# A gated linear-attention decoder layer in fp32 precision on one core: GpSimd no longer waits for VectorE's split before it prepares the decay exponents

## The chip, the cores and the metric

The kernel runs on one core of a Trainium2 chip. The metric is device time in microseconds (us) of one execution, lower is better. The kernel before took 2335.89 us, the median of three runs (2335.0 to 2343.12).

## The reference, cut to what matters

```python
# x: (4, 512, 512); attention: H = 16 heads, DK = 96, DV = 192
q, k, v = (causal_conv_silu(h @ W) for W in (Wq, Wk, Wv))      # h = layernorm(x)
q, k = l2norm(q) * DK ** -0.5, l2norm(k)
beta = sigmoid(h @ Wb) * 2
g = -exp(A_log) * softplus(h @ Wa + dt_bias)
...
def step(S, inp):                                              # over the 512 tokens
    q_t, k_t, v_t, g_t, b_t = inp
    S = S * exp(g_t)
    delta = (v_t - einsum('bhk,bhkv->bhv', k_t, S)) * b_t
    S = S + einsum('bhk,bhv->bhkv', k_t, delta)
    o = einsum('bhk,bhkv->bhv', q_t, S)
...
x = x + (o * rsqrt(mean(o * o) + eps) * norm_weight * silu(h @ Wg)) @ Wo
x = x + choose_two_sets_and_mix(layernorm(x), ctx_2048, itok)
x = x + bit_linear(silu(bit_linear(y, gate)) * bit_linear(y, val), out)   # y = layernorm(x)
```

The token recurrence is computed in chunks of 128 tokens. Within a chunk the decays between two tokens are exponentials of differences of running sums of g.

## The kernel before, in words

There are three stages. The first normalizes x, the third chooses the sets and does the feed-forward part. The second, `stage_delta_rule`, is the long one: 64 steps numbered n = 0 to 63, one for each of 16 heads and 4 chunks of 128 tokens, each for all four batch rows at once. `c` is the chunk of the step, n modulo 4. In a step the kernel works on four steps' data at once: it projects and convolves q, k, v of step n + 2 (`projection`, `tap0`, `conv`, `tanh`, `silu`), prepares and inverts the triangular matrix of step n + 1, runs the state update of step n, and normalizes, gates and projects the output of step n - 1.

Each engine has its own instruction list, written out by hand, and executes it strictly in order; semaphores (`then_inc`, and `wait_ge` or `past`) order the engines against each other. `past(engine, name, value)` waits until the semaphore has reached the value, and does nothing for a value of zero or less.

These are the pieces around the change:

- GpSimd (`pool`), in a step: `key_decay` makes UB, Em and kinv (L762 to L769); then four products K2 (L823, one of 128x96 for each batch row); then `exponents(n + 2)` (L742), two products of a 128x512 constant with the high and the low half of the f16 pair that holds g, into the one buffer `Gm`; then `values` (L777), two products that make V of the next step from the transposed tokens, after a wait for all four of ScalarE's token copies (`tok_read`); then `epsq` (L832).
- `exponents` itself first waits for `dif_done`, the signal of the two matmuls on TensorE (`exponent_sums`, L884) that read the last `Gm`. They run near the start of a step; the new `Gm` is read near the start of the step after it.
- VectorE: after the state terms `d_V` (L1559) comes `gated`, four products of d_O, the row scale and d_gate into d_on (L1616); `recursion(0)` to `(3)`, four tiny steps on 32 partitions (L1524 to L1534); `silu(0)` (L1473 into d_yv); then `low` (L1624, L1625), which subtracts the f16 high half in d_ohl from d_on and signals `low_ready`; then two taps of the next convolution (L1452), `recursion(4)` (L1536), the third tap, for c other than 2 a small correction (L1458), and `recursion(5)` (the first two L1545).
- In a step with c = 0 VectorE also splits a weight tile (`low_g`, L1441) ahead of `gated`; with c = 2 another (`low_a`, L1436) after `recursion(6)`.
- ScalarE: after the second token copy (L1255) comes `high` (L1350), which waits for d_on and writes the f16 high half; then `tap0(1)` (L1206); then `copy_yj` (L1296), which copies a triangular block that TensorE's `x_join` (L960) waits for; and so on.
- TensorE: ..., `x_join`, `queries` times the state, the fourth token transpose (L875), `turn_output` (L999), which waits for `low_ready` and transposes d_ohl, the rest of the third projection (L859), the output matmuls (L1019), the gates (L974) and the update (L986). The L986 that works on d_V writes a bank that `add_x` (L1630) on VectorE must have read.

The line that the change touches stands in GpSimd's `step`, between K2 and `exponents`:

```python
if st.project:
    past(pool, "low_ready", n)
    exponents(n + 2)
```

Of the kernel before, what the change touches and what calls it, by code (L numbers as in the profile page):

```python
# [79 lines left out]
def over(ap, axis, n):  # L80

    a = ap.unsqueeze(axis)
    shape = list(a.shape)
    shape[axis] = n
    return a.broadcast_to(shape)
# [387 lines left out]
def set_scale(nc, pool, s, c, smv, var, rstd, half):  # L473

    nc.gpsimd.tensor_scalar(var[:, c, :], smv[:, :, :].rearrange("p (b c) m -> p c b m", c=CH)[:, c, :, 1], LN_EPS, None,
                            ALU.add).then_inc(s["var_ready"], 1)
    pool.wait_ge(s["var_ready"], c + 1)
    nc.gpsimd.tensor_tensor(rstd[:, c, :], var[:, c, :], half[:, :], ALU.pow).then_inc(s["rstd_ready"], 1)


def set_weights(nc, pool, s, c, eg, first, second, wt):

    pool.wait_ge(s["eg_ready"], c + 1)
    pool.wait_ge(s["hit_ready"], 2 * c + 2)
    nc.gpsimd.tensor_tensor(second, second, over(eg, 2, NSET), ALU.mult).then_inc(s["wt_ready"], 1)
    pool.wait_ge(s["wt_ready"], 2 * c + 1)
    nc.gpsimd.tensor_tensor(wt[:, c, :, :], first, second, ALU.add).then_inc(s["wt_ready"], 1)
# [39 lines left out]
def stage_delta_rule(nc, io, keep):  # L527
# [6 lines left out]
    with ExitStack() as ctx:  # L534
# [72 lines left out]
        def chosen(c):  # L607
            flat, hits = st[:, c * 320:], y[c][:, :, :].rearrange("p b t -> p (b t)")
            return {"score": flat[:, 0:B * NSET].rearrange("p (b n) -> p b n", b=B),
                    "top": flat[:, 256:288].rearrange("p (b e) -> p b e", b=B),  # L610
                    "topi": st[:, 640 + c * 32:672 + c * 32].bitcast(U32).rearrange("p (b e) -> p b e", b=B),
                    "idx": flat[:, 288:296].rearrange("p (b e) -> p b e", b=B),
                    "gap": flat[:, 296:300], "eg": flat[:, 300:304], "den": flat[:, 304:308],
                    "first": [hits[:, 0:256].rearrange("p (b n) -> p b n", b=B)] * 2,
                    "second": [hits[:, 256:512].rearrange("p (b n) -> p b n", b=B)] * 2}
# [8 lines left out]
        def hold(eng, sem, value):  # L624

            eng.wait_ge(sem, value)
            if not isinstance(value, int):
                eng.sem_inc(held[str(eng.engine)], 1)

        def past(eng, name, value):  # L630

            if not isinstance(value, int):
                if eng.engine == nc.vector.engine:
                    eng.wait_ge(s[name], value)
                else:
                    hold(eng, s[name], value)
            elif value > 0:
                eng.wait_ge(s[name], value)
# [98 lines left out]
        def _(pool):  # L737
            def exponents(n):

                past(pool, "dif_done", n)  # L740
                for w in range(2):
                    nc.gpsimd.tensor_tensor(Gm[:, w, :, :], over(U, 1, B), over(gh[:, w, n, :], 2, P), ALU.mult).then_inc(s["Gm_ready"], 1)  # L742

            def carry(st):

                m = st.n + 2
                past(pool, "tail_done", 3 * m)
                for back in (3, 2, 1):
                    w = over(over(cw[:, st.kp, :, 3 - back], 2, B), 3, back)
                    if back == 3:  # L750
                        nc.gpsimd.tensor_tensor(corr[:, :, :, :], tail[st.pm][:, :, :, :], w, ALU.mult).then_inc(s["corr_ready"], 1)
                        continue
                    past(pool, "corr_ready", 5 * carried(m) + 5 - 2 * back)
                    nc.gpsimd.tensor_tensor(share[:, :, :, 0:back], tail[st.pm][:, :, :, 3 - back:], w, ALU.mult).then_inc(s["corr_ready"], 1)
                    past(pool, "corr_ready", 5 * carried(m) + 6 - 2 * back)
                    nc.gpsimd.tensor_tensor(corr[:, :, :, 0:back], corr[:, :, :, 0:back], share[:, :, :, 0:back], ALU.add).then_inc(s["corr_ready"], 1)

            def key_decay(m, q):

                hold(pool, s["Dn_ready"], 5 * m + 5)  # L760
                past(pool, "Em_ready", m)
                nc.gpsimd.tensor_tensor(UB[:, :, :], over(cst[:, C_NU:C_NU + P], 1, B), over(Dn[:, :], 2, P), ALU.mult).then_inc(s["kappa_done"], 1)  # L762
                nc.gpsimd.tensor_scalar(sse[:, :], nsse[:, :], -1.0, None, ALU.mult).then_inc(s["kappa_done"], 1)
                past(pool, "E_ready", m + 1)
                hold(pool, s["kappa_done"], 4 * m + 2)
                past(pool, "PT_ready", m - 1)
                nc.gpsimd.tensor_tensor(Em[q][:, :, :], E[:, :, :], UB[:, :, :], ALU.mult).then_inc(s["Em_ready"], 1)
                past(pool, "V_ready", m)
                nc.gpsimd.tensor_tensor(kinv[:, :], sse[:, :], phalf[:, :], ALU.pow).then_inc(s["kappa_done"], 1)  # L769
# [18 lines left out]
            def step(st):  # L788
                n, m, c = st.n, st.n + 1, st.c
                if st.output:  # L790

                    past(pool, "ssq_done", B * n)
                    nc.gpsimd.tensor_scalar(ms[:, :], sso[:, :], NORM / DV, None, ALU.mult).then_inc(s["r_ready"], 1)  # L793
                    past(pool, "r_ready", 3 * n - 2)
                    nc.gpsimd.tensor_tensor(ms[:, :], ms[:, :], epsq[st.pm][:, :], ALU.add).then_inc(s["r_ready"], 1)
                    past(pool, "r_ready", 3 * n - 1)
                    past(pool, "on_ready", B * n - B)
                    nc.gpsimd.tensor_tensor(rn[:, :], ms[:, :], mhalf[:, :], ALU.pow).then_inc(s["r_ready"], 1)
                if n >= NS - 1:
                    for at in (0, 1) if n == NS - 1 else (2,):  # L800
                        past(pool, "aggr", B * at + B)
                        set_scale(nc, pool, ss_, at, smv, set_var, set_rstd, mhalf)
                if n == NS:
                    for at in range(2):
                        t = chosen(at)
                        set_weights(nc, pool, ss_, at, t["eg"], t["first"][0], t["second"][0], wt)
                if st.project:
                    if st.cp:
                        carry(st)
                    if not st.recur:  # L810
                        exponents(n + 2)
                    if n == -2:
                        pool.wait_ge(s["set_in"], 96)
                        nc.gpsimd.tensor_copy(bqb[:, :, :], over(bq[:, :], 2, P)).then_inc(s["const_ready"], 1)
                if st.turn:
                    key_decay(m, st.pm)
                if st.recur:

                    past(pool, "su_done", 2 * n)
                    if n == 0:  # L820
                        pool.wait_ge(s["set_done"], 1)
                    for i in range(B):
                        nc.gpsimd.tensor_scalar(K2[:, i, :], tok[st.p][:, i, K_AT:K_AT + DK], Em[st.p][:, i, P - 1:P], None,  # L823
                                                ALU.mult).then_inc(s["K2_ready"], 1)
                    if st.project:
                        past(pool, "low_ready", n)
                        exponents(n + 2)
                if st.turn:

                    values(m, st.pm)  # L830
                    past(pool, "ss_done", B * m + B)
                    nc.gpsimd.tensor_scalar(epsq[st.pm][:, :], ss[:, :], EPS, EPS * DK * NORM, ALU.add, ALU.mult).then_inc(s["kappa_done"], 1)  # L832
                if c == 0 and st.recur:
                    low_o(st.k, st.wk)
                if n == 0:
                    pool.wait_ge(s["set_read"], 3)
                    nc.gpsimd.tensor_scalar(sc[:, NEG, :, :], sc[:, EG, :, :], -1.0, None, ALU.mult).then_inc(s["const_ready"], 1)

            nc.gpsimd.memset(ones[:, :], 1.0).then_inc(s["const_ready"], 1)
            hold(pool, s["const_ready"], 15)  # L840
            all_steps(step)

        @block.tensor
# [1467 lines left out]
```

## Time and profile before

| | before |
|---|---|
| median of 3 runs | 2335.89 us (2335.0 to 2343.12) |
| the profiled execution, its own time | 2335.0 us |
| its span, first to last instruction | 2333.2 us |
| mean granted TensorE clock | 0.984 |
| TensorE matmuls busy | 2250.7 us, 96% |
| VectorE busy | 2074.5 us, 89% |
| ScalarE busy | 1450.8 us, 62% |
| GpSimd busy | 1062.0 us, 46% |

PE is TensorE, PEld its weight loads, DVE VectorE, ACT ScalarE, POOL GpSimd. Times in a timeline are us from the start of the span. A line of it is one instruction or a run of equal ones ("x4"), with the time from the first one's start to the last one's end; in square brackets is how long the engine was idle before it, and who released it.

### The profile page before, as it was taken

The numbers are of one execution on the slowest core, as the hardware profiler recorded it, in microseconds if no ns is written. First come the engines' busy times: TensorE is split into PE (matmuls) and PEld (weight loads), VectorE is DVE, ScalarE is ACT, GpSimd is POOL, SyncE is SP. The second block draws the span as 40 slices with busy tenths as digits, with TensorE's granted clock in tenths as the row PEclk, the third lists the DMA queues.
The fourth block names the chain that finished last, engine by engine and source line by source line (L and its number), as shares of the span: only waits on it lengthen the run. The fifth ranks groups of instructions, "written<-read, shape, count | busy, mean of one in ns | idle before, by whom it ended". The sixth has DMA issues, their size and how long they took to land. (4 is left out here: it accounts for less than half of the span.)

```text
span 2333.2 us, 55508 instructions
## 1 busy us (share of the span) xinstructions
PE 2250.7 (96%) x19873; PEld 1573.5 (67%) x19896; DVE 2074.5 (89%) x4579; ACT 1450.8 (62%) x3955; POOL 1062.0 (46%) x1542
## 2 busy tenths in 40 slices
PE   5899999999999999999999999999999999888998
PEld 3577777777777767777767677777777677763454
DVE  8999999999999999999999998999999989657876
ACT  5566666666666666666666766665656565434665
POOL 3535444444535454535354544445354535214554
PEclk8999999999999999999999999999999999898999
DMA  5211122222212112222221222221111111011000
GB/s 143 62 36 51 50 56 55 57 55 55 51 51 49 53 48 66 63 65 62 56 53 50 65 63 66 64 65 39 34 37 34 22 39 23 17 59 83 24 24 28
DMA packets 289390, 120.76 MB, mean 52 GB/s; under 512 B 211510, under 2 KB 267094, under 8 KB 288604
## 3 DMA queue, kind: packets, MB, share of 16 engines
q1 hardware_dynamic: 289116, 117.21, 19.2%
q8 instruction: 159, 2.61, 0.5%
q14 instruction: 115, 0.94, 0.1%
HBM read 85.42 MB, written 31.74 MB: 50 GB/s over the span
## 5 line engine op out<-in xcount | busy, mean ns | idle before, releaser
L1452 DVE SCALAR_TENSOR_TENSOR d_y<-bank,d_cw,d_y 128x508 f32<-128x508 f32 (+2 forms) x576 | 421.4, 732 | 6.1 <-ACT d_y L1206 1.2
L793 POOL TENSOR_SCALAR d_ms<-d_sso 128x4 f32<-128x4 f32 x64 | 14.5, 226 | 563.8 <-ACT d_junk L1345 563.8
L742 POOL TENSOR_TENSOR d_Gm<-cst,gh 128x512 f16<-128x512 f32 x128 | 131.0, 1044 | 216.5 <-DVE d_ohl L1625 214.5
L1630 DVE SCALAR_TENSOR_TENSOR x<-bank,x 128x512 f32<-128x512 f32 x256 | 172.0, 676 | 43.7 <-PE bank L1019 43.7
L1330 ACT ACTIVATE d_thg<-bank 128x384 f32<-128x384 f32 x128 | 62.2, 486 | 205.1 <-PE bank L974 202.8
L1206 ACT ACTIVATE d_y<-bank,d_cw 128x512 f32<-128x512 f32 x192 | 131.2, 684 | 88.3 <-PE bank L859 86.6
L777 POOL TENSOR_TENSOR d_V<-d_tok,d_kinv 128x640 f32<-128x640 f32 (+1 forms) x128 | 132.0, 1051 | 49.4 <-issue 47.3
L823 POOL TENSOR_SCALAR d_K<-d_tok,d_Em 128x96 f32<-128x96 f32 x256 | 152.1, 609 | 0.1
L1255 ACT ACTIVATE d_tok<-bank 128x384 f32<-128x384 f32 x256 | 125.5, 490 | 36.2 <-PE bank L875 32.3
L1213 ACT ACTIVATE d_th<-d_y 128x512 f32<-128x512 f32 x192 | 122.1, 636 | 39.8 <-DVE d_y L1458 29.8
L1473 DVE SCALAR_TENSOR_TENSOR d_yv<-d_th,d_y 128x512 f32<-128x512 f32 x128 | 89.0, 696 | 52.3 <-ACT d_th L1213 44.5
L1019 PE MATMUL bank<-d_wo1h,d_onT 128*128 128x512 f16 x384 | 131.0, 382 | 3.0 <-ACT d_onT L1357 2.8
L1019 PE MATMUL bank<-d_wo0h,d_onT 128*128 128x512 f16 x384 | 130.1, 380 | 0.2
L1545 DVE TENSOR_TENSOR d_prod<-d_Lb,d_XTb 32x64 f32<-32x64 f32 (+1 forms) x192 | 127.0, 685 | 0.1
L974 PE MATMUL bank<-d_wgh,hhi 128*128 128x192 f16 x1024 | 126.5, 246 | 0.0
L974 PE MATMUL bank<-d_wgl,hhi 128*128 128x192 f16 x1024 | 126.5, 246 | 0.0
L974 PE MATMUL bank<-d_wgh,hlo 128*128 128x192 f16 x1024 | 126.5, 246 | 0.0
L1335 ACT ACTIVATE d_Dl<-bank 128x384 f32<-128x384 f32 x128 | 62.7, 491 | 100.7 <-PE bank L986 100.7
L1345 ACT ACTIVATE d_junk<-d_O 128x192 f32<-128x192 f32 x256 | 89.6, 351 | 53.6 <-DVE d_O L1576 39.5
L986 PE MATMUL bank<-d_V,d_XT 128*128 128x192 f32 x512 | 109.8, 337 | 8.2 <-DVE x L1630 8.2
L832 POOL TENSOR_SCALAR d_epsq<-d_ss 128x4 f32<-128x4 f32 x64 | 25.6, 400 | 199.7 <-ACT d_sq L1308 199.7
L1886 POOL TENSOR_TENSOR f_zv<-f_zv,f_zg 128x512 f32<-128x512 f32 x64 | 83.9, 1312 | 56.3 <-ACT f_zg L2049 34.1
(340 smaller groups left out, 6924.5 us busy)
## 6 DMA issues: line engine op xcount, KB each, us to landing
lt_blocks<-d_LT SPq DMA_DIRECT2D x64, 256.0 KB, 2.5
d_fw<-turned_gate_w SPq DMA_DIRECT2D x32, 256.0 KB, 3.1
d_XT<-x_blocks SPq DMA_DIRECT2D x128, 64.0 KB, 2.3
d_X<-x_blocks SPq DMA_DIRECT2D x128, 64.0 KB, 2.4
d_fw<-turned_val_w SPq DMA_DIRECT2D x32, 256.0 KB, 3.0
d_fw<-turned_out_w SPq DMA_DIRECT2D x32, 256.0 KB, 2.9
d_st<-in_L_attn_Wg_dram SPq DMA_DIRECT2D x16, 384.0 KB, 4.1
ternary<-d_ft SPq DMA_DIRECT2D x48, 128.0 KB, 2.1
```

Source lines behind the costliest of these rows:

```text
L742: nc.gpsimd.tensor_tensor(Gm[:, w, :, :], over(U, 1, B), over(gh[:, w, n, :], 2, P), ALU.mult).then_inc(s["Gm_ready"], 1)
L777: last = nc.gpsimd.tensor_tensor(V[q][:, :, lo:hi], tok[q][:, :, at:at + hi - lo], over(kinv[:, :], 2, hi - lo), ALU.mult)
L823: nc.gpsimd.tensor_scalar(K2[:, i, :], tok[st.p][:, i, K_AT:K_AT + DK], Em[st.p][:, i, P - 1:P], None, ALU.mult).then_inc(s["K2_ready"], 1)
L974: last = nc.tensor.matmul(bank[(4, 7)[pair]][:, i * DV:(i + 1) * DV], x[:, k, tile * P:(tile + 1) * P], wg[w][:, k, :], start=(e == 0), st ...
L986: last = nc.tensor.matmul(bank[at][0:rows, i * DV:(i + 1) * DV], lhsT(e), rhs(e), start=True, stop=True)
L1019: last = nc.tensor.matmul(bank[(4, 7, 6, 5)[i]][:, :], o, w, start=(e == 0), stop=(e == len(terms) - 1))
L1206: nc.scalar.activation(y[(st.p + j) % 2][:, :, :].rearrange("p b t -> p (b t)"), bank[(st.p + j) % 2][:, :], ACT.Copy, scale=cw[:, ds(st.k ...
L1213: nc.scalar.activation(th[:, :, :], y[(st.p + j) % 2][:, :, :], ACT.Tanh).then_inc(s["tanh_done"], 1)
L1255: nc.scalar.activation(tok[st.pm][:, i, :], bank[2][:, 0:QKV], ACT.Copy).then_inc(s["tok_read"], 1)
L1452: nc.vector.scalar_tensor_tensor(out=yy[:, :, tap:], in0=pp[:, :, 0:P - tap], scalar=cw[:, ds(st.kp, 1), t, 3 - tap], in1=yy[:, :, tap:], ...
L1545: last = nc.vector.tensor_tensor(prods.rearrange("q (g j i k) -> q g j i k", g=g, j=w, i=w)[:, e], over(left[:, e], 2, w), over(right[:, e ...
L1630: nc.vector.scalar_tensor_tensor(out=xs, in0=bank[(4, 7, 6, 5)[i]][:, :], scalar=1.0 / (SO * SW), in1=xs, op0=ALU.mult, op1=ALU.add).then_ ...
```

## The change

One wait is taken out. In a step with a projection (n up to 61) GpSimd no longer waits, between K2 and the two Gm products, for VectorE's `low` of the same step. Nothing else is different.

```diff
                     if st.project:
-                        past(pool, "low_ready", n)
                         exponents(n + 2)
```

`exponents` still waits for `dif_done`, so that Gm is not overwritten while TensorE reads it. In step 0 the wait was for zero and so was no wait in the kernel before either.

## Rows read from the trace of the kernel before

**Rows 1.** The page: busy time, share of the span, instructions
```profile
PE 2250.7 (96%) x19873; PEld 1573.5 (67%) x19896; DVE 2074.5 (89%) x4579; ACT 1450.8 (62%) x3955; POOL 1062.0 (46%) x1542
```

**Rows 2.** Who waited for whom: total us, times, longest us
```profile
POOL d_Gm L742 <- DVE d_ohl L1625: 214.5, 60, 6.5
...
PEld bank L960 <- ACT d_YJ L1296: 14.0, 61, 0.4
PEld bank L986 <- DVE x L1630: 11.7, 15, 1.1
```

**Rows 3.** Timeline of step 0, GpSimd and VectorE: start, us, instruction
```profile
93.20 2.56 POOL L742 TENSOR_TENSOR d_Gm<-cst,gh 128x512 f16<-128x512 f32 x2
...
93.35 0.91 DVE L1534 TENSOR_TENSOR d_part<-d_XTb 32x8 f32<-32x8 f32 x1
94.18 0.67 DVE L1473 SCALAR_TENSOR_TENSOR d_yv<-d_th,d_y 128x512 f32<-128x512 f32 x1
94.79 1.51 DVE L1452 SCALAR_TENSOR_TENSOR d_y<-bank,d_cw,d_y 128x508 f32<-128x508 f32 x2
96.21 0.15 DVE L1536 TENSOR_TENSOR d_XTb<-d_XTb,d_part 32x8 f32<-32x8 f32 x1
```

**Rows 4.** Timeline of step 52 (c = 0), GpSimd
```profile
1695.16 3.20 POOL L823 TENSOR_SCALAR d_K<-d_tok,d_Em 128x96 f32<-128x96 f32 x4
1700.23 2.04 POOL L742 TENSOR_TENSOR d_Gm<-cst,gh 128x512 f16<-128x512 f32 x2 [1.87 <-DVE d_ohl L1625]
1702.22 1.72 POOL L777 TENSOR_TENSOR d_V<-d_tok,d_kinv 128x640 f32<-128x640 f32 x2
```

**Rows 5.** Timeline of step 52, VectorE
```profile
1698.23 0.16 DVE L1534 TENSOR_TENSOR d_part<-d_XTb 32x8 f32<-32x8 f32 x1
1698.52 0.69 DVE L1473 SCALAR_TENSOR_TENSOR d_yv<-d_th,d_y 128x512 f32<-128x512 f32 x1
1699.13 0.68 DVE L1624 TENSOR_TENSOR d_ohl<-d_on,d_ohl 128x512 f16<-128x512 f32 x1
1699.73 0.42 DVE L1625 TENSOR_TENSOR d_ohl<-d_on,d_ohl 128x256 f16<-128x256 f32 x1
...
1701.50 0.79 DVE L1536 TENSOR_TENSOR d_XTb<-d_XTb,d_part 32x8 f32<-32x8 f32 x1
...
1702.97 0.54 DVE L1458 TENSOR_TENSOR d_y<-d_y,d_corr 128x12 f32<-128x12 f32 x1
```

**Rows 6.** Timeline of step 52, TensorE
```profile
1701.01 0.83 PE L999 MATMUL bank<-d_idh,d_ohl 128*128 128x128 f16 x12
...
1711.65 0.92 PE L986 MATMUL bank<-d_V,d_XT 128*128 128x192 f32 x4 [0.78 <-DVE x L1630]
```

**Rows 7.** Timeline of step 53 (c = 1), VectorE, then TensorE
```profile
1729.23 0.69 DVE L1624 TENSOR_TENSOR d_ohl<-d_on,d_ohl 128x512 f16<-128x512 f32 x1 [0.53 <-ACT d_ohl L1350]
...
1732.02 0.83 PE L999 MATMUL bank<-d_idh,d_ohl 128*128 128x128 f16 x12
```

**Rows 8.** Timeline of step 54 (c = 2), GpSimd, VectorE, ScalarE
```profile
1755.35 2.04 POOL L823 TENSOR_SCALAR d_K<-d_tok,d_Em 128x96 f32<-128x96 f32 x4
...
1756.99 1.42 DVE L1616 SCALAR_TENSOR_TENSOR d_on<-d_O,d_rn,d_gate 128x192 f32<-128x192 f32 x4
...
1759.87 0.83 ACT L1350 ACTIVATE d_ohl<-d_on 128x768 f16<-128x768 f32 x1
```

**Rows 9.** Timeline of step 55 (c = 3), GpSimd, VectorE, ScalarE
```profile
1787.24 2.05 POOL L823 TENSOR_SCALAR d_K<-d_tok,d_Em 128x96 f32<-128x96 f32 x4
...
1788.89 1.41 DVE L1616 SCALAR_TENSOR_TENSOR d_on<-d_O,d_rn,d_gate 128x192 f32<-128x192 f32 x4
...
1796.28 0.17 DVE L1458 TENSOR_TENSOR d_y<-d_y,d_corr 128x12 f32<-128x12 f32 x1
...
1791.56 0.83 ACT L1350 ACTIVATE d_ohl<-d_on 128x768 f16<-128x768 f32 x1
```

## The prediction

> **What bounds the kernel now.** I read the page first. TensorE's matmuls are busy for 96% of the span and VectorE for 89% [rows 1]: in the long second stage TensorE is the bound, and nearly any time it loses there comes out in the end, while VectorE is close enough to become the bound in places. Then the list of who waited for whom. GpSimd stood for 214.5 us in 60 waits, 3.6 us each, exactly at the wait that is removed [rows 2]. That looks like much, but GpSimd is an engine with slack, so the question is who would notice if Gm came earlier, and who would notice how. The same list names the places where TensorE waits for others in most steps: 61 times for ScalarE's copy d_YJ, and 15 times for VectorE's addition into x [rows 2]. Last come timelines of one step of each kind, c = 0, 1, 2 and 3, because the order of the engines' work differs with c, and of step 0, the only step in the trace in which Gm already follows K2 at once.
>
> **Nobody waits for Gm.** In step 52 it is made from 1700.23 to 1702.27 [rows 4], but the two matmuls that read it come near the start of the next step, more than 10 us later: TensorE's L986 of step 52 at 1711.65 [rows 6] still comes ahead of them. V, the next thing on GpSimd, starts at 1702.22, right behind Gm, when c = 0 [rows 4]; there it could start a little earlier, up to the last token copy, but its reader also belongs to the next step. So the benefit on dependencies is nothing: 214.5 us of waiting is moved on GpSimd, not taken from the path.
>
> **What the move does.** The two Gm products now start as K2 ends. That puts them beside other VectorE instructions, and the trace shows that this matters. The tiny L1536, 0.15 us in step 0 where Gm was long done [rows 3], takes 0.79 us in step 52, where it starts at 1701.50 inside the second Gm product (1701.2 to 1702.27), and it ends with it [rows 4, 5]. The convolution taps L1452, which take one operand from PSUM, run through beside Gm (1.51 us for two) [rows 3]. In step 0, L1534 starts 0.15 us after Gm and takes 0.91 us instead of the 0.16 us of step 52 [rows 3, 5]: released at 93.20 + 0.90. The silu that follows gets its turn, and now it is Gm's second product that waits: the pair takes 2.56 us, 0.52 us over the usual 2.04 [rows 3, 4]. I read three rules out of this: a Gm product keeps a VectorE instruction with two operands in SBUF out for 0.90 us from its start; such an instruction keeps Gm out until about 0.15 us before its own end; and the two engines take turns, the one that waits longer first.
>
> The Trainium skill (SBUF — State Buffer, "Who interferes with whom") says the same of the pair: a VectorE instruction with two SBUF inputs contends with a GpSimd instruction that reads SBUF, and the second to issue fully blocks until the first finishes. By that rule the change is worth what its new neighbours cost; without it (bandwidth shared, or no conflict) it would be worth nothing. The rows above agree with the first.
>
> The old neighbours of Gm are two taps, which don't mind, and L1536, which loses 0.79 - 0.15 = 0.64 us. The new ones are d_on (L1616), the tiny recursions, silu and low: all with two operands in SBUF. Both Gm products now block, about 2 x 0.9 us, and then it depends on c who passes that on.
>
> **c = 0.** K2 ends at 1698.36, so Gm starts at about 1698.33 (in step 0 it starts just as K2 ends). It lets silu (1698.52) go at 1699.23, +0.71. Gm's second product waits for silu until 1699.77 and holds until 1700.67. The first half of low is ready at 1699.84 and waits for that: 1700.67 in place of 1699.13, +1.54 [rows 4, 5]. Low ends at 1701.69 in place of 1700.15, and TensorE, which starts L999 at 1701.01 [rows 6], stands for about 0.75 us. But 10 us later TensorE stands 0.78 us for VectorE's x anyway, in each of the 15 such steps [rows 2, 6]; so its loss at L999 disappears into that wait, and what counts is how late VectorE is by then. VectorE is 1.54 us late, gets back 0.64 us at L1536, and 0.37 us at L1458, which V holds for 0.54 instead of 0.17 us today [rows 5, 9] and which would now come after V. That leaves 0.53 us; V may hold L1536 for up to some 0.3 us instead, so I take 0.6 us. Bounds: 0.3 us, and 0.9 us when nothing but L1536 is given back.
>
> **c = 3.** d_on is four instructions, each 0.33 us after the last and 0.41 us long (1.41 us together) [rows 9]. K2 ends at 1789.29. Gm's first product waits for the second d_on (from 1789.22, so out at 1789.48) and holds until 1790.38; the third d_on runs, out at 1790.64; the second product holds until 1791.54; and the fourth d_on starts there, not at 1789.88, and ends at 1791.95, not 1790.30. ScalarE's `high` needs it and starts at 1791.56 today; it can start no earlier than 1791.95, +0.4 us, and with an allowance of 0.1 us for the signal I take +0.5 us. ScalarE executes in order and has d_YJ two instructions behind `high`, and TensorE waits for d_YJ in 61 steps [rows 2]. So this 0.5 us reaches TensorE whole. VectorE's own lateness at low is hidden, as in c = 1 below.
>
> **c = 2.** The same with other times: K2 ends at 1757.39, the second d_on holds from 1757.32, and the fourth ends at 1760.06 instead of 1758.41. `high` goes from 1759.87 to 1760.06 or, with the same allowance, 1760.16: +0.3 us [rows 8]. Bounds for both: 0 when K2 is late enough or the blocks shorter, 0.8 us when the fourth d_on has to wait once more.
>
> **c = 1.** `high` is fed in time, because only the last d_on is still running when K2 ends. VectorE loses at most 1.8 us, of which 0.53 us is idle time ahead of low today [rows 7]: +1.27 us. Low ends at 1731.52 instead of 1730.25 (1.02 us for the pair, as in [rows 5]), and TensorE wants it at 1732.02 [rows 7]: hidden. Of the 1.27 us, 0.64 come back at L1536. I take 0; bound 0.3 us.
>
> **The sum.** There are 15 steps each with c = 0, 2 and 3 that change (4 to 60, 2 to 58, 3 to 59), and 16 with c = 1. 15 x (0.6 + 0.3 + 0.5) = 21 us. The profiled execution took 2335.0 us, 0.9 under the median of 2335.89, so 2356 us, 0.9% slower. Bounds: 15 x 0.3 = 5 us from below if only the smallest c = 0 term holds; 15 x (0.9 + 0.8 + 0.8) + 16 x 0.3 = 42 us from above. About 0.5%, 11.7 us, is what a measurement of this kernel can tell from no change.
>
> **Rivals.**
>
> *Moved and hidden.* The blocks are there, but the slack of VectorE and ScalarE takes them: the total block is only 2 x 0.9 against 0.64 us now, and VectorE idles before low for 0.5 us and more when c is not 0. Against it: ScalarE's queue is gapless from the token copy to d_YJ, and TensorE waits for it. Left is 0 to 0.6 us in c = 0: 2335 to 2344 us, within 0.5%.
>
> *Faster.* If a Gm beside d_on and silu cost them nothing (long f32 products may leave gaps that L1536 did not find), VectorE would only win: 0.64 us per step at L1536. TensorE would cash that where it waits for VectorE, in 15 steps of 0.78 us: -0.64 x 15 = -10 us, 2325 us. It decides from the point where the new blocks sum to less than 0.64 us per step. Step 0, where one block alone took 0.75 us, speaks against it.
>
> *Much slower.* If the engines did not take turns, or if TensorE's loss at L999 came on top of its wait for x and VectorE's lateness in c = 1 reached it: a whole 1.8 us less the 0.64 in each of 61 steps, 71 us, 2406 us. Silu's prompt turn in step 0 speaks against it.
>
> **How the numbers follow.** The forecast, 2344 to 2377 us, gets 0.68; hidden 0.20; faster 0.06; much slower 0.06. The predicted time is 2356. A range from 2337 to 2376 leaves out the faster rival, the much slower one and the lowest part of hidden: 2 in 10. Faster by over 0.5% gets 0.04, since that rival lies mostly within 0.5%; of the forecast, times under 2347.6 us have some 0.08 and count as the same with hidden and the rest of faster: 0.28; slower 0.68.
>
> **What would show it.** After the change: no wait of Gm for L1625; L1536 at 0.15 us in most steps; silu or low of c = 0 stretched to over 1.3 us; two d_on of c = 2 and 3 at about 1.2 us; `high` waiting for d_on in those steps; TensorE idle before L999 when c = 0; V starting earlier when c = 0. The prediction is wrong if Gm is blocked by VectorE rather than the reverse (Gm pairs far over 2.04 us, VectorE unstretched), or if TensorE makes up the 0.3 to 0.5 us at d_YJ at a later wait.

## The result, and the profile after

| | before | after |
|---|---|---|
| median of 6 runs of each | 2344.58 us (2335.0 to 2347.24) | 2363.6 us (2356.55 to 2368.23) |
| profiled execution, its own time | 2335.0 us | 2356.22 us |
| its span | 2333.2 us | 2354.4 us |
| mean granted TensorE clock | 0.984 | 0.985 |

The ratio is 1.0091, with a 95% interval from 1.0076 to 1.0107: slower by 0.9%, some 21 us, as forecast. It rests on more executions (28 of the kernel after) than the medians of the table, which alone would give 1.0081, 19 us. The two profiled executions, with nearly the same granted clock, are 21.2 us apart. As an absolute time 2363.6 us lies 7.6 us above the forecast 2356, because the median of the kernel before was 8.7 us higher here than the 2335.89 us that the forecast started from. One execution of the kernel before and one of the kernel without the wait in c > 0, further down, took over 7850 us; both are left out of every ratio and median here.

In the kernel after, lines below L825 have numbers smaller by one: what was L1616 is L1615. The page's first part, of the kernel after:

```profile
PE 2258.2 (96%) x19896; PEld 1571.7 (67%) x19896; DVE 2128.2 (90%) x4579; ACT 1458.2 (62%) x3955; POOL 1072.1 (46%) x1542
```

Against [rows 1] VectorE is busy for 53.7 us more with the same 4579 instructions. Nothing was added to its list, so the same instructions take longer. The page's groups say which (busy time, mean ns of one, idle time before):

```profile
L1615 DVE SCALAR_TENSOR_TENSOR d_on<-d_O,d_rn,d_gate 128x192 f32<-128x192 f32 x256 | 158.5, 677 | 0.0
...
L1472 DVE SCALAR_TENSOR_TENSOR d_yv<-d_th,d_y 128x512 f32<-128x512 f32 x128 | 98.9, 772 | 52.2 <-ACT d_th L1212 44.5
...
L1623 DVE TENSOR_TENSOR d_ohl<-d_on,d_ohl 128x512 f16<-128x512 f32 x64 | 55.5, 867 | 4.0 <-ACT d_ohl L1349 4.0
...
L1535 DVE TENSOR_TENSOR d_XTb<-d_XTb,d_part 32x8 f32<-32x8 f32 x64 | 12.4, 194 | 0.0
...
L742 POOL TENSOR_TENSOR d_Gm<-cst,gh 128x512 f16<-128x512 f32 x128 | 142.7, 1137 | 0.1
```

In the trace of before the same groups took 91.4, 89.0, 44.2, 49.3 and 131.0 us, the first and the fourth of them as

```profile
L1616 DVE SCALAR_TENSOR_TENSOR d_on<-d_O,d_rn,d_gate 128x192 f32<-128x192 f32 x256 | 91.4, 415 | 0.0
...
L1536 DVE TENSOR_TENSOR d_XTb<-d_XTb,d_part 32x8 f32<-32x8 f32 x64 | 49.3, 770 | 0.0
```

So d_on lost 67.1 us, silu 9.9, the first half of low 11.3, and L1536 got 36.9 back: 51.4 of the 53.7 us. Two smaller groups nearly cancel: the copy of `recursion(0)` lost 9.8 us, and the small products of `recursion(5)` got 10.0 back. The Gm products themselves are 11.7 us longer. And the waits (us in total, times, longest):

```profile
PEld bank L959 <- ACT d_YJ L1295: 25.1, 61, 1.1
...
PEld bank L998 <- DVE d_ohl L1624: 17.7, 16, 5.3
...
PEld bank L985 <- DVE x L1629: 10.2, 15, 0.9
...
POOL d_V L777 <- issue: 254.0, 62, 9.5
```

GpSimd's 214.5 us of waiting [rows 2] did not vanish: they now stand ahead of V, where it was 47.3 us before. TensorE waits for d_YJ 61 times as before, but 11.1 us longer in sum, and 16 times for low instead of twice; its wait for x is nearly the same.

Step 52 (c = 0) in the timeline of after, GpSimd, VectorE, TensorE, against [rows 4 to 6]:

```profile
1713.50 3.23 POOL L823 TENSOR_SCALAR d_K<-d_tok,d_Em 128x96 f32<-128x96 f32 x4
1716.69 2.48 POOL L742 TENSOR_TENSOR d_Gm<-cst,gh 128x512 f16<-128x512 f32 x2
1720.14 1.61 POOL L777 TENSOR_TENSOR d_V<-d_tok,d_kinv 128x640 f32<-128x640 f32 x2 [0.96 <-issue]
...
1716.88 1.40 DVE L1472 SCALAR_TENSOR_TENSOR d_yv<-d_th,d_y 128x512 f32<-128x512 f32 x1
1718.20 1.52 DVE L1623 TENSOR_TENSOR d_ohl<-d_on,d_ohl 128x512 f16<-128x512 f32 x1
1719.65 0.41 DVE L1624 TENSOR_TENSOR d_ohl<-d_on,d_ohl 128x256 f16<-128x256 f32 x1
...
1721.41 0.35 DVE L1535 TENSOR_TENSOR d_XTb<-d_XTb,d_part 32x8 f32<-32x8 f32 x1
...
1722.45 0.17 DVE L1457 TENSOR_TENSOR d_y<-d_y,d_corr 128x12 f32<-128x12 f32 x1
...
1720.12 0.84 PE L998 MATMUL bank<-d_idh,d_ohl 128*128 128x128 f16 x12 [0.64 <-DVE d_ohl L1624]
...
1730.69 0.92 PE L985 MATMUL bank<-d_V,d_XT 128*128 128x192 f32 x4 [0.70 <-DVE x L1629]
```

Gm starts as K2 ends. Silu takes 1.40 us instead of 0.69, low 1.52 instead of 0.68: one product holds each. L1536 and L1458 are shorter by 0.44 and 0.37 us.

Step 55 (c = 3), GpSimd, VectorE, ScalarE, TensorE, against [rows 9], and then d_on and `high` of two steps with c = 1, first step 53 and then step 57:

```profile
1809.09 2.16 POOL L742 TENSOR_TENSOR d_Gm<-cst,gh 128x512 f16<-128x512 f32 x2
...
1808.72 3.08 DVE L1615 SCALAR_TENSOR_TENSOR d_on<-d_O,d_rn,d_gate 128x192 f32<-128x192 f32 x4
...
1811.83 0.84 ACT L1349 ACTIVATE d_ohl<-d_on 128x768 f16<-128x768 f32 x1 [0.33 <-DVE d_on L1615]
1813.28 0.38 ACT L1295 ACTIVATE d_YJ<-bank 64x256 f32<-64x256 f32 x1
...
1813.71 0.68 PE L959 MATMUL bank<-d_XT,d_YJ 128*64 128x64 f32 x8 [0.28 <-ACT d_YJ L1295]
...
1743.63 2.06 POOL L823 TENSOR_SCALAR d_K<-d_tok,d_Em 128x96 f32<-128x96 f32 x4
1745.65 2.16 POOL L742 TENSOR_TENSOR d_Gm<-cst,gh 128x512 f16<-128x512 f32 x2
...
1744.84 3.18 DVE L1615 SCALAR_TENSOR_TENSOR d_on<-d_O,d_rn,d_gate 128x192 f32<-128x192 f32 x4
...
1748.05 0.84 ACT L1349 ACTIVATE d_ohl<-d_on 128x768 f16<-128x768 f32 x1 [0.55 <-DVE d_on L1615]
...
1871.34 2.15 POOL L742 TENSOR_TENSOR d_Gm<-cst,gh 128x512 f16<-128x512 f32 x2
...
1870.32 2.27 DVE L1615 SCALAR_TENSOR_TENSOR d_on<-d_O,d_rn,d_gate 128x192 f32<-128x192 f32 x4
...
1872.88 0.83 ACT L1349 ACTIVATE d_ohl<-d_on 128x768 f16<-128x768 f32 x1
```

In step 55 four d_on take 3.08 us in place of 1.41: two holds. `high`, which waited for nothing before, now stands for d_on, and TensorE stands for d_YJ. With c = 1 the steps differ. Step 53 looks like step 55; in step 57 Gm comes 0.2 us later, only the last d_on is held, and `high` waits for nothing. Four of the fourteen heads have a c = 1 step like 53 (steps 5, 25, 49 and 53), ten one in which only the last d_on is held.

For all steps I took the time from the first matmul of L923 in a step to the first in the next, as medians over 14 heads (n = 4 to 59), the same for every kernel below:

| kernel (ratio to before, 95% interval) | c = 0 | c = 1 | c = 2 | c = 3 |
|---|---|---|---|---|
| before | 29.13 | 31.51 | 31.70 | 31.10 |
| after, 1.0091 (1.0076 to 1.0107) | 29.83 | 31.83 | 31.91 | 31.46 |
| Gm only filled, early, 0.9964 (0.9943 to 0.9984) | 28.72 | 31.51 | 31.51 | 31.10 |
| Gm only filled, wait kept, 0.9974 (0.9957 to 0.9992) | 28.99 | 31.51 | 31.51 | 31.10 |
| wait gone, c = 0 alone, 1.0050 (1.0028 to 1.0072) | 29.86 | 31.51 | 31.70 | 31.10 |
| wait gone, c > 0 alone, 1.0076 (1.0050 to 1.0103) | 29.15 | 31.83 | 31.90 | 31.43 |
| Gm made twice, 1.0392 (1.0368 to 1.0417) | 31.06 | 32.95 | 33.22 | 32.21 |
| c = 0 alone, low ahead of silu, 1.0049 (1.0033 to 1.0065) | 29.82 | 31.51 | 31.70 | 31.10 |
| d_YJ ahead of high, wait kept, 1.0117 (1.0090 to 1.0143) | 29.14 | 31.73 | 32.91 | 31.32 |
| the same, wait gone in c > 0, 1.0069 (1.0043 to 1.0094) | 29.14 | 31.74 | 32.30 | 31.33 |
| wait kept, recursion(4) later, 1.0011 (0.9992 to 1.0029) | 29.20 | 31.51 | 31.67 | 31.10 |
| Gm ahead of K2 in c > 0, 0.9991 (0.9973 to 1.0009) | 29.15 | 31.51 | 31.51 | 31.10 |
| Gm last on GpSimd, 1.0000 (0.9981 to 1.0018) | 28.77 | 31.79 | 31.51 | 31.10 |

From before to after the fourteen heads take 19.9 us more of the span's 21.2 us.

The medians of c = 1 have to be read with care. In the kernel before eight of those steps take 31.51 us and six 31.78, so a median can move by 0.3 us when few steps do. The means are 31.62 us before, 31.85 after and 31.74 without the wait in c > 0. Ten of the fourteen steps lose 0 to 0.06 us from before to after; the four named above lose 0.93, 0.45, 0.96 and 0.57 us. With the other c the loss is in nearly every head (means 0.68, 0.20 and 0.32 us for c = 0, 2 and 3).

### The profile page after: what moved, and what is told of

The parts are those of the page before. It is cut to its first block and busy times, and to the rows that moved or that the text cites. A ratio compares the mean times of both kernels' runs of the same rounds, so it can differ in the third digit from the quotient of the medians.

```text
span 2354.4 us, 55470 instructions
## 1 busy us (share of the span) xinstructions
PE 2258.2 (96%) x19896; PEld 1571.7 (67%) x19896; DVE 2128.2 (90%) x4579; ACT 1458.2 (62%) x3955; POOL 1072.1 (46%) x1542
## 3 DMA queue, kind: packets, MB, share of 16 engines
HBM read 85.42 MB, written 31.74 MB: 50 GB/s over the span
## 5 line engine op out<-in xcount | busy, mean ns | idle before, releaser
L777 POOL TENSOR_TENSOR d_V<-d_tok,d_kinv 128x640 f32<-128x640 f32 (+1 forms) x128 | 131.1, 1044 | 256.2 <-issue 254.0
L1615 DVE SCALAR_TENSOR_TENSOR d_on<-d_O,d_rn,d_gate 128x192 f32<-128x192 f32 x256 | 158.5, 677 | 0.0
L1472 DVE SCALAR_TENSOR_TENSOR d_yv<-d_th,d_y 128x512 f32<-128x512 f32 x128 | 98.9, 772 | 52.2 <-ACT d_th L1212 44.5
L742 POOL TENSOR_TENSOR d_Gm<-cst,gh 128x512 f16<-128x512 f32 x128 | 142.7, 1137 | 0.1
L1544 DVE TENSOR_TENSOR d_prod<-d_Lb,d_XTb 32x64 f32<-32x64 f32 (+1 forms) x192 | 117.4, 635 | 0.1
```

The costliest lines, as they stand in the source:

```text
L777: last = nc.gpsimd.tensor_tensor(V[q][:, :, lo:hi], tok[q][:, :, at:at + hi - lo], over(kinv[:, :], 2, hi - lo), ALU.mult)
L1544: last = nc.vector.tensor_tensor(prods.rearrange("q (g j i k) -> q g j i k", g=g, j=w, i=w)[:, e], over(left[:, e], 2, w), over(right[:, e ...
L1615: nc.vector.scalar_tensor_tensor(out=on[:, i, :], in0=O[:, i, :], scalar=rn[:, i:i + 1], in1=gate[:, i, :], op0=ALU.mult, op1=ALU.mult).th ...
```

## The experiments

**Is it the operands, or Gm's time?** Both products become fills of the same size, of which the first goes into a spare buffer; the wait is gone. The decay exponents are left out, so this kernel does less than the reference. If Gm being early were itself the cost, it would stay; if reading beside VectorE is the cost, it goes.

```diff
-                    nc.gpsimd.tensor_tensor(Gm[:, w, :, :], over(U, 1, B), over(gh[:, w, n, :], 2, P), ALU.mult).then_inc(s["Gm_ready"], 1)
+                    nc.gpsimd.memset(spareG[:, w, :, :], 0.0)
+                    nc.gpsimd.memset(Gm[:, w, :, :], 0.0).then_inc(s["Gm_ready"], 1)
...
-                        past(pool, "low_ready", n)
```

> The changed kernel, with each Gm product replaced by two write-only fills of the same 128x512 f16 size (one into a spare tile, one into Gm); the decay exponents are left out, so the output is not the reference's. GpSimd is busy about as long at the same place, but reads nothing from SBUF. Theory (VectorE is kept out by Gm's reads): d_on, silu and low are not stretched, L1536 takes 0.15 us, and the time is at or a little below the kernel before, 0.99 to 1.00 of it. Rival (it is GpSimd being busy early, its writes, or the missing order between the engines): still slower, 1.005 to 1.01.

Measured: 2335.44 us, 0.9964 (0.9943 to 0.9984). Timeline of its step 54 (c = 2), GpSimd and VectorE:

```profile
1748.43 0.52 POOL L743 MEMSET d_spareG<- 128x512 f16 x1
1748.90 0.52 POOL L744 MEMSET d_Gm<- 128x512 f16 x1
...
1748.07 1.43 DVE L1617 SCALAR_TENSOR_TENSOR d_on<-d_O,d_rn,d_gate 128x192 f32<-128x192 f32 x4
1749.42 0.95 DVE L1525 COPY d_XTb<-d_Lb 32x8 f32<-32x8 f32 x1
...
1751.82 0.69 DVE L1625 TENSOR_TENSOR d_ohl<-d_on,d_ohl 128x512 f16<-128x512 f32 x1
...
1754.20 0.15 DVE L1537 TENSOR_TENSOR d_XTb<-d_XTb,d_part 32x8 f32<-32x8 f32 x1
```

d_on, low and L1537 are unstretched with a GpSimd that writes at the same place. Not all of the recursion is: its first instruction, the copy L1525, takes 0.95 us instead of 0.16, behind the d_on that `high` waits for. TensorE's wait for d_YJ is 14.0 us, as in before. So it is not that Gm is early. A fill is also half as long as a product, so this alone doesn't separate reading from duration. The trace of before doesn't either: the last K2, which reads SBUF too and is as short as a fill (0.52 us), begins ahead of the first d_on in [rows 8], and the four d_on take their usual 1.42 us.

**The same in the kernel before, wait kept.** The exponents are left out here too. It tells what the wait itself is worth, and how much of the gain above was merely the lighter Gm.

> The kernel before, wait kept, with the same write-only fills in place of the Gm products (the exponents are left out). With the wait removed the fills gave 0.9964. Theory (the wait itself is worth nothing, only Gm's reads cost): 0.996 to 0.997 here too. If being early on GpSimd is worth something by itself: 0.999 to 1.000 here.

Measured: 2338.42 us, 0.9974 (0.9957 to 0.9992). The two differ by 0.1%, with intervals that overlap. By the steps, taking the wait out beside fills gains 0.27 us with c = 0 and nothing with the others: the wait itself is worth little. What both kernels gain, 0.19 us in c = 2 and 0.14 us in c = 0 even when fills come at the old place, I put down to the collision of Gm with L1536, which takes 0.15 us in both.

**Which steps lose?** The wait is taken out in c = 0 alone, and in the others alone (a wait for zero is none).

```diff
-                        past(pool, "low_ready", n)
+                        past(pool, "low_ready", n if c else 0)
```

> The wait is removed only in steps with c = 0. Theory: TensorE stands 0.76 us longer at L999 in 15 steps and gets back under 0.1 us at L986: +10 us, ratio 1.004. Rival (loss at L999 disappears in the later wait for x, as the prediction had it): +5 us or less from VectorE's lateness alone, 1.002; other rival (all steps alike): 1.0023.

> The wait is removed only in steps with c = 1, 2, 3. Theory: high on ScalarE comes 0.15 to 0.35 us later, d_YJ with it, and TensorE waits for it: about 0.7 us per head, +11 us, ratio 1.0045. If the loss sat at L999 in c = 0 alone: 1.000. The two partial removals should add up to the whole change, 1.009.

Measured: 2351.7 us, 1.0050 (1.0028 to 1.0072), and with `0 if c else n` 2356.69 us (median of five), 1.0076 (1.0050 to 1.0103). Each loses only in the steps where its wait is gone, by about the amounts of the kernel after: 0.73 us in c = 0; 0.12, 0.19 and 0.30 us in the means of the others, where the kernel after loses 0.23, 0.20 and 0.32. Of the four c = 1 steps that lose 0.4 us and more after, only steps 5 and 25 do so here; steps 49 and 53 lose only when the wait is gone in c = 0 too.

The ratios don't add up (0.50% and 0.76% against 0.91%), but the heads do: 9.1 and 9.9 us against 19.9. The second ratio is high for another reason. Of 24 executions of the kernel before in the same batch, 9 have a granted clock of 0.984 or more, with a median of 2337.1 us, and 15 a lower one, with 2345.2 us. All five of this kernel have 0.981 or 0.982, and against those 15 they are 11.5 us longer, near what its heads give. In its profile the part after the last step's start takes 306.3 us at a granted clock of 0.915, in that of before 296.6 us at 0.953. The result of c = 0 can't tell TensorE's stall at L999 from VectorE's lateness, since both sums lie near it.

The two waits of TensorE part in the same way. The list of waits without the wait in c = 0 alone:

```profile
PEld bank L999 <- DVE d_ohl L1625: 17.6, 16, 5.3
...
PEld bank L960 <- ACT d_YJ L1296: 14.0, 61, 0.4
```

and without it in the others alone:

```profile
PEld bank L960 <- ACT d_YJ L1296: 23.0, 61, 1.0
```

**More of it.** The kernel after with each product made twice, first into a spare buffer.

```diff
+                    nc.gpsimd.tensor_tensor(spareG[:, w, :, :], over(U, 1, B), over(gh[:, w, n, :], 2, P), ALU.mult)
                     nc.gpsimd.tensor_tensor(Gm[:, w, :, :], over(U, 1, B), over(gh[:, w, n, :], 2, P), ALU.mult).then_inc(s["Gm_ready"], 1)
```

> The changed kernel with each Gm product made twice, the first time into a spare tile: four products follow K2 in place of two. It measures the suspected cost by doubling it. Theory (each product keeps VectorE out once, about 0.9 us): 1.8 us more lateness in every step, of which almost nothing is hidden any more, since the slack at low is used up by the first two: at least twice the cost of the change, 1.02 to 1.05. If the cost of the change came from something that happens once (the order of the two engines), 1.009 to 1.012.

Measured: 2438.76 us, 1.0392 (1.0368 to 1.0417), where GpSimd still idles for half the time. A head's four steps are 6.0 us longer than before, against 1.4 us with the product made once (means). The first holds are partly taken by slack: VectorE is busy for 53.7 us more, and the kernel is some 21 us longer. Those on top are paid whole: 70.9 us more of VectorE's busy time, and 75 us. Its waits:

```profile
PEld bank L961 <- ACT d_YJ L1297: 48.9, 61, 2.4
...
PE bank L1000 <- DVE d_ohl L1626: 38.8, 30, 5.0
...
PE bank L987 <- DVE x L1631: 22.0, 29, 1.1
```

**c = 0: TensorE's stall at L999, or VectorE's lateness?** The wait is gone in c = 0 alone, and there low comes ahead of silu, so that TensorE gets d_ohl nearly on time while VectorE loses as much.

```diff
-                                 rec(2), rec(3), (P_, lambda: silu(st, 0)), (O_, low), (P_, lambda: conv(st, 1, 1)), (P_, lambda: conv(st, 1, 2)), rec(4),
+                                 rec(2), rec(3), (O_ and c == 0, low), (P_, lambda: silu(st, 0)), (O_ and c > 0, low), (P_, lambda: conv(st, 1, 1)), (P_, lambda: conv(st, 1, 2)), rec(4),
```

> The wait is removed with c = 0 only, and in those steps VectorE does low ahead of silu. VectorE has the same work and the same two blocks, but low, which TensorE's L999 waits for, comes between the two instead of behind both: L999 should start about 0.2 us late instead of 0.8 us. If what costs is how late VectorE is at x (the prediction's step): the same as with the wait gone for c = 0 in the old order, step 29.8 us, ratio 1.005. If TensorE's stand at L999 is what costs: step 29.3 us, ratio 1.001.

Measured: 2354.73 us, 1.0049 (1.0033 to 1.0065), the same as without the reordering. L999 starts at 10.48 us into the step instead of 11.09 (10.26 before), x at 15.23 in both. The waits show where the saved stall went:

```profile
PE bank L986 <- DVE x L1630: 15.5, 15, 1.3
```

against, without the reordering,

```profile
PE bank L986 <- DVE x L1630: 6.7, 14, 0.7
```

TensorE gains 0.6 us at one wait and loses it at the next. VectorE's lateness at x is the cost.

**c > 0: is it d_YJ behind `high`?** On ScalarE `copy_yj` goes ahead of `high` for c > 0, once with the wait kept and once with it gone for c > 0.

```diff
-                                 (R_, copy_y32), (P_, lambda: tanh(st, 0)), (R_, copy_x64), (T_, lambda: tokens(st, 1)), (O_, high), (P_, lambda: tap0(st, 1)),
-                                 (R_, copy_yj), (R_, lambda: read_qs(0)), (T_, lambda: tokens(st, 2)), (R_, join), (R_, lambda: read_qs(1)),
+                                 (R_, copy_y32), (P_, lambda: tanh(st, 0)), (R_, copy_x64), (T_, lambda: tokens(st, 1)), (O_ and st.c == 0, high), (P_, lambda: tap0(st, 1)),
+                                 (R_, copy_yj), (O_ and st.c > 0, high), (R_, lambda: read_qs(0)), (T_, lambda: tokens(st, 2)), (R_, join), (R_, lambda: read_qs(1)),
```

> The kernel before, waits kept, but in steps with c = 1, 2, 3 ScalarE copies d_YJ ahead of high instead of behind it. It is the base for the next run. TensorE waits 0.15 to 0.2 us for d_YJ in these steps, so 0 to 0.6 us per head may be won; low gets later by 0.8 us, under TensorE's slack at L999: ratio 0.996 to 1.001.

> The same order on ScalarE, and the wait removed in steps with c = 1, 2, 3. Theory: the loss of these steps reaches TensorE only through high standing ahead of d_YJ in ScalarE's queue, so here it is gone: within 3 us of the run with this order and the waits kept, where in the old order it cost 10 to 11 us per kernel (head 124.2 us against 123.4). Rival (VectorE's lateness reaches TensorE by another way): 8 us or more over the run with the waits kept.

Measured: 2369.27 us, 1.0117 (1.0090 to 1.0143), and 2358.2 us, 1.0069 (1.0043 to 1.0094). Both expectations fell. The base was misjudged: `high` starts at 9.78 us into a step instead of 8.32, low is late with it, and VectorE is late at x, a wait of TensorE that grows from 8.2 to 22.2 us. And the second kernel was expected within 3 us of the first, but is 11 us faster (6.2 us by the fourteen heads). Step by step the pair answers the question still. Timeline of the second one's step 54, VectorE and ScalarE:

```profile
1773.38 3.08 DVE L1616 SCALAR_TENSOR_TENSOR d_on<-d_O,d_rn,d_gate 128x192 f32<-128x192 f32 x4
...
1778.59 0.69 DVE L1624 TENSOR_TENSOR d_ohl<-d_on,d_ohl 128x512 f16<-128x512 f32 x1 [0.65 <-ACT d_ohl L1350]
...
1777.31 0.38 ACT L1296 ACTIVATE d_YJ<-bank 64x256 f32<-64x256 f32 x1
1777.72 0.84 ACT L1350 ACTIVATE d_ohl<-d_on 128x768 f16<-128x768 f32 x1
```

d_on is stretched to the same 3.08 us, but nothing on TensorE's way to d_YJ waits for it: L960 starts at 10.28 us into a step with the wait kept or gone (10.61, 10.42 and 10.61 us for c = 1, 2 and 3 where `high` stands ahead and the wait is gone in c > 0). Taking the wait out now costs 0.01 us in the medians of c = 1 and c = 3 (0.00 and 0.08 in the means, where it cost 0.12 and 0.30), and gains 0.61 us in c = 2. There L1536 takes 0.15 us instead of 0.79 in every step, VectorE reaches x 0.61 us earlier, and TensorE's wait for x falls from 22.2 to 13.8 us. The loss in c > 0 runs through `high` to d_YJ.

**Can the old collision be avoided?** With all waits kept, `recursion(4)` is moved behind the third tap, out of Gm's way.

```diff
-                                 rec(2), rec(3), (P_, lambda: silu(st, 0)), (O_, low), (P_, lambda: conv(st, 1, 1)), (P_, lambda: conv(st, 1, 2)), rec(4),
-                                 (P_, lambda: conv(st, 1, 3)), rec(5), rec(6), (True, lambda: lows(1)), (P_, lambda: silu(st, 1)), rec(7),
+                                 rec(2), rec(3), (P_, lambda: silu(st, 0)), (O_, low), (P_, lambda: conv(st, 1, 1)), (P_, lambda: conv(st, 1, 2)),
+                                 (P_, lambda: conv(st, 1, 3)), rec(4), rec(5), rec(6), (True, lambda: lows(1)), (P_, lambda: silu(st, 1)), rec(7),
```

> The kernel before, waits kept, with VectorE's L1536 (recursion 4) moved behind the third convolution tap. Theory: the Gm pair now lies beside taps alone, L1536 takes 0.15 us instead of 0.79, VectorE has 0.64 us more in every step; TensorE cashes it where it waits for x in c = 0: up to 15 x 0.64 = 10 us, ratio 0.996, at least 0.999. Rival (V or another GpSimd instruction then keeps L1536 or the correction out, or TensorE's wait for x hangs on something else): 1.000.

Measured: 2343.45 us, 1.0011 (0.9992 to 1.0029). The expectation of a gain fell. Timeline of its step 52, GpSimd and VectorE:

```profile
1702.62 1.62 POOL L777 TENSOR_TENSOR d_V<-d_tok,d_kinv 128x640 f32<-128x640 f32 x2
...
1702.79 1.12 DVE L1458 TENSOR_TENSOR d_y<-d_y,d_corr 128x12 f32<-128x12 f32 x1
1703.83 0.15 DVE L1536 TENSOR_TENSOR d_XTb<-d_XTb,d_part 32x8 f32<-32x8 f32 x1
```

L1536 is down to 0.15 us, and L1458, which now meets V, is up from 0.54 to 1.12 us. The hold found another victim.

**Two other places for Gm.** For c > 0 ahead of K2, to lie beside the taps and d_V, which take one operand from PSUM; and in all steps last on GpSimd, behind a recursion of the second half of the step.

```diff
+                    if st.project and c:
+                        exponents(n + 2)
...
-                    if st.project:
+                    if st.project and c == 0:
                         past(pool, "low_ready", n)
```

> In steps with c = 1, 2, 3 the Gm products go ahead of K2, beside the taps and d_V on VectorE, which take one operand from PSUM; with c = 0 the wait and the place of before. Theory: no instruction of VectorE is held by Gm in those steps, high is in time, L1536 takes 0.15 us; of that TensorE can use only what the write-only run showed with c = 2, 0.17 us per head: ratio 0.998 to 1.000. If being early on GpSimd cost anything by itself, over 1.003.

Measured: 2342.8 us, 0.9991 (0.9973 to 1.0009). Gm was expected to be clear of d_on and is not everywhere: in c = 1 the first d_on takes 1.02 us, yet the last ends early enough that `high` starts at 8.33 us into the step, as before; c = 2 wins 0.19 us.

```diff
-                    if st.project:
-                        past(pool, "low_ready", n)
-                        exponents(n + 2)
...
+                    if st.project and st.recur:
+                        past(pool, "rec_done", 13 * m + 12)
+                        exponents(n + 2)
```

> In every step Gm is made last, behind epsq and a wait for recursion 11, beside an addition into x, a reduction, taps and the gate on VectorE, none of which reads two operands from SBUF. Nothing is left out. Theory: the same time as the write-only run, ratio 0.996 (heads of 123.05 us), as all of Gm's collisions are gone. Rival (low_o, which then runs later in steps with c = 0, or GpSimd itself in the next step becomes late; or TensorE waits for Gm at L884): 1.00 or more.

Measured: 2344.62 us, 1.0000 (0.9981 to 1.0018), not the 0.996 that was expected. It wins 0.36 us in c = 0 and 0.19 us in c = 2, and gives 0.28 us back in c = 1 (0.21 in the mean). By its timeline GpSimd has 2 us of products ahead of the weight work of c = 0, and in the step after it K2 and d_on start later (d_on at 6.4 us into step 53 instead of 5.8). None of these full kernels is measurably faster than the kernel before.

## Why the prediction was right, point by point

- **Nobody waits for Gm.** Right: 214.5 us of waiting moved to V (from 47.3 to 254.0 us). With Gm reduced to fills, taking the wait out gains 0.1%, which is inside the intervals.
- **The three rules.** Right in their effect, shown by the stretched instructions of after and by the unstretched ones beside fills. Silu of c = 0 was forecast at +0.71 us (measured 1.40 - 0.69 = 0.71), low's own stretch at 0.83 us (1.52 - 0.68 = 0.84), and both d_on of c = 2 and 3 at about 1.2 us (1.27 and 1.19). Only the order was off: not the third and fourth d_on are held but the second and third. Gm got its first turn ahead of the second d_on; the total, 3.08 us for four, is the same as if it had not.
- **c = 0, 0.6 us.** Measured 0.70. VectorE's low ended 1.60 us later (forecast 1.54). L1458 gave back the 0.37 us; L1536 gave back 0.44 instead of 0.64 us, since V holds it for the rest, as the allowance had it. That TensorE's stall at L999 is not what costs, but VectorE's lateness at x, was argued in the prediction and is shown by low ahead of silu.
- **c = 3, 0.5 us.** Measured 0.36 (0.32 in the mean): the right path at a smaller size. `high` came 0.45 us later (0.39 from the holds and about half of the allowance of 0.1 us for the signal), and L960 0.36 us later, so L960 had some 0.1 us of slack behind d_YJ.
- **c = 2, 0.3 us.** Measured 0.21, with `high` 0.24 us late and L960 0.15.
- **c = 1, 0 us.** Right for ten heads and wrong for four, 0.23 us in the mean, which is under the bound of 0.3. In the ten, only the fourth d_on is held, as in step 57, `high` starts when it did or 0.13 us later, and the step loses at most 0.06 us. The sentence "`high` is fed in time, because only the last d_on is still running when K2 ends" was read from step 53 alone and fails in the other four. In steps 5 and 25 K2 ended before the third d_on in the trace of before already. In steps 49 and 53 it ends 0.2 us earlier after the change, before the fourth. There two d_on are held, `high` comes 0.5 to 1.1 us later, and the steps lose 0.45 to 0.96 us in the same way as c = 3. The prediction looked with c = 1 for VectorE's lateness at low, which is indeed hidden.
- **The sum.** 1.4 us for a head, and 1.42 measured by the means of the steps (0.68, 0.23, 0.20 and 0.32): c = 0 and four steps of c = 1 replaced what c = 2 and 3 fell short. The result is 21.2 us in the profiled executions, where 21 were forecast; that it is this near is partly luck, since these errors cancel.
- **The rivals.** Moved and hidden: excluded by the interval, and by the steps with c = 2 and 3, which lose in nearly every head. Faster: what it counted on, L1536, came (36.9 us of VectorE's time), but the new holds are 88 us. Much slower: the engines do take turns, and the losses at L999 and at x don't add up.

The Trainium skill (SBUF — State Buffer, "Who interferes with whom") has a VectorE instruction with two SBUF inputs contend with a GpSimd instruction that reads SBUF, but not with one that only writes it. The d_on stretched from 1.41 to 3.08 us by two products agrees with it, and so do the unstretched d_on beside fills (1.43 us). The K2 products read SBUF as well, and the d_on beside the last of them stays at 0.43 us in step 54 of before, which that rule would not have: what a pair costs has to be measured.

What stays open is why a product of 1.04 us holds d_on and a K2 of 0.52 us does not, and whether a product longer than a fill but without a read would hold VectorE; that was not tried.

## What to carry to other kernels

A wait of an idle engine can be a placement: before taking it out, list what will run beside the moved instructions, and look for pairs that stretch each other, in the durations of the neighbours and not in idle times. A hold costs what the held instruction feeds has no slack for, so follow each victim to the next consumer of the bounding engine, in every kind of step, and in more than one step of each kind: the one step read for c = 1 was a poor guide to four of fourteen. Four instructions in a row are exposed as long as the last of them hasn't started. Moving a hold from one victim to another gains only where the new one has slack.

## What the runs showed of the hardware that was not expected

- A GpSimd fill of 128x512 f16, which reads nothing, left four d_on with two SBUF operands at 1.43 us, but a VectorE copy of 32x8 f32 beside two fills took 0.95 us instead of 0.16. In the kernel after the same copy takes 1.00 us beside the second product in nine of the fourteen steps with c = 1.
- A GpSimd product of 128x96 by a scalar (K2, 0.52 us), which reads SBUF, left the d_on that began inside it at 0.43 us.
- GpSimd gets its turn between two back-to-back VectorE instructions: in c = 2 and 3 the product starts 0.37 and 0.38 us after the first d_on (medians), which is not lengthened (0.44 us).
- The price is not proportional: twice the products cost 4.2 times as much (6.0 against 1.4 us a head).
